# First attention: a conditioning slice's reciprocal computed by logarithm, exponential and one Newton step in place of VectorE's reciprocal instruction

## The chip, the cores and the metric

One program on one core of one Trainium2 chip. The core's engines are TensorE (PE), VectorE (DVE), ScalarE (ACT), GpSimd (POOL) and SyncE (SP), each with its own instruction stream, kept in step by semaphores. The metric is the time of one execution on the device in microseconds (us), as the median over the runs.

## The reference

The program is two layers over a batch of B = 4 sequences of T = 256 tokens with C = 256 channels. Each layer is an attention and a mixture-of-experts block, and ahead of each of these four stands a conditioning. All four conditionings have the same form, and the change touches only it:

```python
decay = exp(-exp(w))[None, :] * (0.5 + 0.5 * tf[:, :, 0])
ek    = exp(minimum(k, 30.0));  ekv = ek * v
a     = a * decay + ekv_t;      b = b * decay + ek_t      # scans, forward and in reverse
euk   = exp(minimum(u + k, 30.0))
num   = nf + nb - ekv + euk * v
den   = df + db - ek + euk
out   = sigmoid(x) * (num / maximum(den, 1e-8)) * (0.8 + 0.2 * tf)
```

Here k = v = a side input of the program, the same for all four, so `num / den` for every conditioning and sequence is known long before the `x` that it gates. `x + attention(conditioned x)` then follows. The first attention has 16 heads; its logits are mixed across heads before the softmax and its probabilities after it, by weights computed per token ("cross head projection").

## The kernel before, in words

**Slices.** A slice is one conditioning i of one sequence b: slice n = 4i + b, 16 in all. Its data are [128 x 512] in fp32 (two channel halves by 256 tokens). `slice_steps` (L971) gives VectorE's work on a slice as a list of steps: `shifted` (u + k, L987), two `forward` scans (L993), two `backward` scans (L999), `own_term` (L1021), `floor` (the maximum with 1e-8, L1033), four `invert` (a RECIPROCAL of 128 x 128 each, L1040) and `finish` (L1045), which writes num * scale * (1/den) into `fac`. ScalarE takes the exponential of `shifted` (`exp_slice`, L611), and GpSimd adds the sums (`sum_slice`, L528 to L533). `condition_batch` (L1079) multiplies `fac` with the sigmoid of x and so makes `xc`, the input of a sequence's attention.

**Who does what when.** Slice 0 is done at the start. Slices 1 to 8 are spread over the first attention, which takes one sequence b at a time: slice 2b+1 (`own`) is begun and finished in sequence b, slice 2b+2 (`following`) is begun at its end and finished in sequence b+1, where it is called `split`. Slices 9 to 15 are done later, in the expert block.

**The loop over pairs of heads.** Within a sequence a loop over p = 0..8 handles heads 2p and 2p+1. It is a software pipeline written out by hand, once in every engine's program. For pair p:

- TensorE: `second_terms` (the mixed logits), `turn` of the pair before (transposes of probabilities, L1916; it waits for `normalise`), `scores` of the next pair (it waits for VectorE's `first_rank`), `values` of the pair before (it waits for `turn_out`).
- VectorE: `first_rank` (L1199), `fold_values` (L1179), `maximum` (L1209), `mix` of the pair before (L1226), the small `invert` of row sums (L1231, waits for `exps`), and then what the dictionary `extra` has for this p: one to three steps of the slices.
- ScalarE: `turn_out` of the pair before (L701), `diagonals_pre` (L659), `exps` (L677, L679; it waits for `maximum`), `second_rank` (L686), `normalise` (L693), and at p = 4 (p = 1 in the first sequence) `exp_slice`.

Every engine runs its instructions in program order, so a wait or a long piece in one engine's pair holds back everything behind it on that engine. After p = 8 comes a sequence's tail: copies of transposed mixed probabilities (L1279, `mixqT`), the rest of slice `own` (`late_own`), the output products (L1285 to L1298), ScalarE's evacuation of values (L738) and the projections of the next sequence. `hidden0` on TensorE is the first product of the next sequence and waits for `xc`.

Function tables: ScalarE's activation functions need a table in the engine; the build puts an ACT_TABLE_LOAD ahead of an activation whose function is not in the loaded one. Before the change there are 12 such loads in the whole program; in the first attention one for the Gelu (L632) and one for the next Exp (L677) per sequence.

Of the kernel before, what the change touches and what calls it, by code (L numbers as in the profile page):

```python
# [15 lines left out]
ALU = mybir.AluOpType  # L16
ACT = mybir.ActivationFunctionType
# [3 lines left out]
B, T, C = 4, 256, 256  # L21
# [4 lines left out]
N0, HD0 = 16, 16  # L26
# [79 lines left out]
def build(nc, d, out, slots0, made0, slots, split1, made1):  # L106
    ctx = ExitStack()
    with ctx:
        def sb(name, *shape, dt=F32):
            return ctx.enter_context(nc.sbuf_tensor(name, [P, *shape], dt))  # L110

        def sem(name):
            return ctx.enter_context(nc.semaphore(name))
# [6 lines left out]
        euk, euv, num, den, backn, backd = (sb(n, CT, T) for n in ("euk", "euv", "num", "den", "backn", "backd"))  # L120
# [144 lines left out]
        c_dve, c_act = sem("cond_dve"), sem("cond_act")  # L265
# [330 lines left out]
        def _(act):  # L596
            st = Steps(act, act_own)
# [10 lines left out]
            def exp_slice(n):  # L608

                act.wait_ge(euk_in, n + 1)  # L610
                act.activation(euk[:], euk[:], ACT.Exp).then_inc(euk_out, 1)  # L611

            exp_slice(0)
            def sigmoid_batch(b):
                if b:
                    act.wait_ge(xc_ready, b)
                act.activation(sig[:], xT[:, :, bass.ds(b * T, T)], ACT.Tanh, scale=0.5).then_inc(sig_ready, 1)
# [18 lines left out]
            for b in range(B):  # L636
                for tt in range(TT):
# [6 lines left out]
                    q, k = (qk[:, tt, n].rearrange("p (n h) -> p n h", h=HD0) for n in range(2))  # L644
# [9 lines left out]
                def diagonals_pre(n):  # L654
                    if n >= 4:
                        act.wait_ge(s_ready, b * N0 + n - 3)
                    for tt in range(TT):
                        for i in range(2):
                            ins = act.activation(diag_pre[:, n % 4, 2 * tt + i], ident[:], ACT.Copy,  # L659
                                                 scale=mixw[:, tt, 1, 2 + i, n:n + 1])  # L660
                    ins.then_inc(dg_pre, 1)
# [7 lines left out]
                def exps(n):  # L669
                    s = n % 2  # L670
                    act.wait_ge(lmax, b * N0 + n + 1)
                    if n >= 2:
                        act.wait_ge(r_ready, b * N0 + n - 1)
                    if n >= 3:
                        act.wait_ge(h_done, b * N0 + n - 2)
                        act.wait_ge(t_ready, b * N0 + n - 2)
                    act.activation(prob[:, n % 3, 0:P], logit[:, s, 0:P], ACT.Exp, bias=nmax[:, s, 0:1], scale=-1.0,  # L677
                                   accum_out=rsum[:, s, 0:1])
                    act.activation(prob[:, n % 3, P:], logit[:, s, P:], ACT.Exp, bias=nmax[:, s, 1:2], scale=-1.0,  # L679
                                   accum_out=rsum[:, s, 1:2]).then_inc(p_exp, 1)  # L680
# [16 lines left out]
                def turn_out(n):  # L697
                    act.wait_ge(t_ready, b * N0 + n + 1)
                    if n >= 4:
                        act.wait_ge(pv_done, b * N0 + n // 4 * 4 - 1)  # L700
                    act.activation(probT[:, n % 4], ps[:, 2 + n % 2, 0:384], ACT.Copy).then_inc(t_read, 1)  # L701
# [6 lines left out]
                for p in range(N0 // 2 + 1):  # L708
                    pair = (2 * p, 2 * p + 1)
                    if p:  # L710
                        turn_out(2 * p - 2)
                        turn_out(2 * p - 1)
                    if 2 * p + 3 < N0:
                        diagonals_pre(2 * p + 3)
                    for n in pair:
                        if n < N0:
                            exps(n)
                    if p == 0:
                        normalise(0)
                        normalise(1)  # L720
                    for n in pair:
                        if n + 2 < N0:
                            second_rank(n + 2)
                    if p == 0:
                        diagonals_pre(4)
                    for n in pair:
                        if p and n < N0:
                            normalise(n)
                            if n % 2 == 0 and n + 4 < N0:
                                diagonals_pre(n + 4)  # L730
                    if p == (4 if b else 1):
                        exp_slice(2 * b + 1)

                exp_slice(2 * b + 2)
                if 0 < b < B - 1:
# [136 lines left out]
            for i in range(2 * B):  # L872
                b, half = divmod(i, 2)
# [73 lines left out]
        def _(dve):  # L947
            st = Steps(dve, dve_own)
# [19 lines left out]
            cs(dve.tensor_tensor(ekv[:, :, 0:T], ek[:, :, 0:T], kT[:, :, 0:T], ALU.mult))  # L968
            cs.settle()

            def slice_steps(n, nth, early=False, first=False):  # L971

# [1 line left out]
                i, b = divmod(n, B)  # L976
                cols = slice(b * T, (b + 1) * T)

                done = {}
# [50 lines left out]
                def floor():  # L1030
                    if not early and not first:
                        dve.wait_ge(sums_out, nth + 1)
                    st(dve.tensor_scalar(den[:], den[:], 1e-8, None, ALU.max))  # L1033
                    done["floor"] = st.last

                def invert(q):
                    if q == 0:
                        dve.wait_ge(*done["floor"])
                    part = den[:, q // 2, (q % 2) * P:(q % 2 + 1) * P]
                    st(dve.reciprocal(part, part))  # L1040
                    done["invert"] = st.last
# [23 lines left out]
                if first:  # L1065
# [2 lines left out]
                            lambda: finish_first(0), lambda: invert(2), lambda: invert(3), lambda: finish_first(1)]  # L1068
                return [*([] if early else [shifted]), lambda: forward(num, ekv), lambda: forward(den, ek),
                        lambda: backward(backn, ekv), lambda: backward(backd, ek),  # L1070
                        *([early_own_term, early_sums] if early else [own_term]), floor, *(lambda q=q: invert(q) for q in range(4)), finish]

            for step in slice_steps(0, 0, first=True):
                step()
# [12 lines left out]
            split = []  # L1087
# [20 lines left out]
            for b in range(B):  # L1108
# [6 lines left out]
                def heads(ap):  # L1115
                    return ap.rearrange("p (n h) -> p n h", h=HD0)
# [28 lines left out]
                for tt in range(TT):  # L1145
                    q, k = heads(qk[:, tt, 0]), heads(qk[:, tt, 1])
# [82 lines left out]
                def invert(n):  # L1229
                    dve.wait_ge(p_exp, b * N0 + n + 1)  # L1230
                    st.tell(dve.reciprocal(rinv[:, n % 2], rsum[:, n % 2]), r_ready, b * N0 + n + 1)  # L1231


                own, following = slice_steps(2 * b + 1, 2 * b + 1), slice_steps(2 * b + 2, 2 * b + 2)
                if b:
                    extra = {1: split[6:8], 2: split[8:11], 3: split[11:12] + own[0:2], 4: own[2:3], 5: own[3:4],
                             6: own[4:6], 7: own[6:8] + following[0:1]}
                else:
                    extra = {0: own[0:1], 1: own[1:2], 2: own[2:3], 3: own[3:4], 4: own[4:5], 5: own[5:6],
                             7: own[6:9] + following[0:1]}  # L1240
                for p in range(N0 // 2 + 1):
                    if p < N0 // 2:
                        first_rank(2 * p)
                        if p:
                            fold_values(2 * p)
                        dve.wait_ge(s_read, b * N0 + 2 * p + 1)
                        first_rank(2 * p + 1)
                        maximum(2 * p)
                        dve.wait_ge(s_read, b * N0 + 2 * p + 2)
                    if p == N0 // 2 and b == 0:  # L1250
                        for step in own[9:12]:
                            step()
                        condition_batch(1, 0, 2)
                    if p:
                        mix(2 * p - 2)
                    else:
                        fold_values(0)
                    if p < N0 // 2:
                        maximum(2 * p + 1)
                        invert(2 * p)  # L1260
                    if p:
                        mix(2 * p - 1)
                    else:
                        fold_values(1)
                    if p < N0 // 2:
                        invert(2 * p + 1)
                    if 0 < p < N0 // 2:
                        fold_values(2 * p + 1)
                    for step in extra.get(p, []):
                        step()  # L1270
                    if p == 3 and 0 < b < B - 1:
                        condition_batch(b + 1, 0, b + 2)

                late_own = own[8:12] if b else []
                for step in late_own[0:1]:
                    step()
                for i in range(2):
# [21 lines left out]
                split = following  # L1299
# [341 lines left out]
            first, middle, last = slice(0, HEAD), slice(HEAD, HEAD + TT), slice(HEAD + TT, TAU)  # L1641
# [17 lines left out]
            for i in range(2 * B):  # L1659
                b, half = divmod(i, 2)  # L1660
# [76 lines left out]
            for kind, which in kinds:  # L1737
                n = which.stop - which.start
# [774 lines left out]
```

## Time and profile before

| | |
|---|---|
| median of 3 runs | 1050.88 us (1050.41 to 1057.42) |
| the profiled execution | 1054.82 us, its span 1053.0 us |
| TensorE / VectorE / ScalarE busy | 913.4 / 797.4 / 572.9 us (87 / 76 / 54% of the span) |
| mean granted TensorE clock | 0.945 |
| first attention | about 20 to 440 us of the span |

The span is what the trace covers; 1.8 us of the execution lie around it. Busy shares are averages over stages with different limits. [...]

### The profile page before, as it was taken

The page shows a single profiled execution, that of the slowest core. Times are in us where ns is not written, and L with a number is a line of the kernel's source. Part 1 is how long each engine was busy: PE and PEld are TensorE (multiplying, and loading weights), DVE is VectorE, ACT ScalarE, POOL GpSimd, SP SyncE. Part 2 cuts the span into 40 slices and gives each one's busy share as a digit, 9 for nine tenths or more (in the row PEclk, how much of TensorE's full clock was granted, in tenths as well). Part 3 has the DMA queues.
Part 4 walks back from the last instruction along what each step waited for, and adds up shares of the span by engine and source line. Part 5 has one row for each costly group of instructions (what it writes and reads, how often), then busy time and mean ns, then how long its engine had stood idle before and what let it go on. Part 6 is the DMA issues. An engine that isn't in the chain of part 4 may idle for free.

```text
span 1053.0 us, 18249 instructions
## 1 busy us (share of the span) xinstructions
PE 913.4 (87%) x6216; PEld 656.6 (62%) x6216; DVE 797.4 (76%) x2089; ACT 572.9 (54%) x1458; POOL 191.2 (18%) x168
## 2 busy tenths in 40 slices
PE   2989988988898889679999999788898998899993
PEld 1777676867686777454566666523333437788983
DVE  7689889988988899984299996557666766366664
ACT  2698489838973798241233332246474761555551
POOL 1102030103001301037344443200000005011111
PEclk9999999989999999779999999969998987799997
DMA  9999950000000000035467784424464544788773
GB/s 247 199 204 237 239 141 1 2 1 1 1 2 1 1 1 2 1 124 177 133 204 242 237 250 135 173 81 164 178 218 160 210 174 138 268 324 295 275 271 130
DMA packets 71452, 153.80 MB, mean 146 GB/s; under 512 B 11439, under 2 KB 53054, under 8 KB 67136
## 3 DMA queue, kind: packets, MB, share of 16 engines
q1 hardware_dynamic: 65696, 139.93, 44.2%
q0 software_dynamic: 5664, 12.71, 3.3%
q8 instruction: 50, 0.82, 0.3%
q14 instruction: 42, 0.34, 0.1%
HBM read 122.09 MB, written 62.19 MB: 175 GB/s over the span
## 4 chain that ended last, share of the span: by engine, by line
PE 53%; DVE 25%; ACT 8%; DMA 6%; issue 5%; POOL 1%; SPq 1%; DVEq 0%; ACTq 0%; POOLq 0%
PE ps L1796 48%; DVE arena L1546 2%; DVE arena L1209 2%; DMA arena<-slots 2%; DVE arena L1199 2%; DVE arena L1226 2%; DMA arena<-split 2%; ACT arena L693 2%; POOL slots L582 1%; ACT arena L659 1%; ACT arena L686 1%; DMA made<-arena 1%; DVE arena L1179 1%; DVE arena L1775 1%; DVE den L1040 1%
## 5 line engine op out<-in xcount | busy, mean ns | idle before, releaser
L1796 PE MATMUL ps<-arena 128*128 128x128 f32 (+15 forms) x4652 | 711.4, 333 | 39.8 <-DVE arena L1199 16.2
L1796 PEld LDWEIGHTS ps<-arena 128*128 128x128 f32 (+7 forms) x4652 | 489.2, 149 | 189.1 <-issue 88.0
L1546 DVE TENSOR_REDUCE arena<-ps 128x4 f16<-128x1024 f32 (+1 forms) x48 | 58.8, 1227 | 52.5 <-PE ps L1796 52.5
L1226 DVE SCALAR_TENSOR_TENSOR arena<-arena 128x128 f32<-128x128 f32 x240 | 91.8, 442 | 0.4
L1773 DVE CAST arena<-arena 128x128 f16<-128x128 f32 (+1 forms) x128 | 33.2, 259 | 62.9 <-ACT arena L919 60.3
L659 ACT ACTIVATE arena<-ident,arena 128x128 f32<-128x128 f32 x256 | 80.2, 392 | 0.0
L824 ACT ACTIVATE arena<-ps 128x1024 f32<-128x1024 f32 x48 | 49.2, 1025 | 45.6 <-PE ps L1796 45.5
L919 ACT ACTIVATE arena<-ps,arena 128x128 f32<-128x128 f32 (+1 forms) x128 | 50.1, 417 | 44.0 <-PE ps L1796 38.8
L562 POOL DMA_INDIRECT made<-arena x47 | 53.0, 1128 | 87.0 <-DVE arena L1459 85.5
L528 POOL TENSOR_TENSOR den<-den,backd 128x512 f32<-128x512 f32 x8 | 11.9, 1482 | 280.7 <-DVE euv L1021 232.6
L1040 DVE RECIPROCAL den<-den 128x128 f32<-128x128 f32 x64 | 57.6, 928 | 0.4
L1199 DVE SCALAR_TENSOR_TENSOR arena<-arena,ps 128x128 f32<-128x128 f32 (+1 forms) x128 | 46.2, 401 | 14.3 <-PE ps L1796 13.9
L582 POOL DMA_INDIRECT slots<-side x16 | 15.6, 973 | 209.6 <-DVE side L1635 205.3
L693 ACT ACTIVATE arena<-arena 128x128 f32<-128x128 f32 (+1 forms) x128 | 49.2, 440 | 0.0
L1179 DVE TENSOR_TENSOR arena<-arena 128x512 f32<-128x512 f32 x64 | 49.0, 766 | 0.0
L1775 DVE TENSOR_TENSOR arena<-arena 128x128 f16<-128x128 f32 (+1 forms) x128 | 45.3, 354 | 4.4
L1796 PE MATMUL ps<-causal,identb 128*128 128x256 bf16 x160 | 36.7, 313 | 12.4 <-DVE arena L1546 9.7
L686 ACT ACTIVATE arena<-arena 128x128 f32<-128x128 f32 (+1 forms) x128 | 47.3, 441 | 0.1
L1576 DVE TENSOR_TENSOR arena<-arena 128x512 f16<-128x512 f32 x64 | 42.4, 683 | 5.8 <-ACT arena L864 5.7
L1916 PE MATMUL ps<-ident,arena 128*128 128x128 f32 x192 | 31.1, 285 | 17.7 <-ACT arena L693 17.1
L1209 DVE CUSTOM_DVE_ANT_0 arena<-arena 128x128 f32<-128x128 f32 (+1 forms) x128 | 46.3, 396 | 0.0
L589 POOL DMA_INDIRECT made<-arena x23 | 22.8, 990 | 128.2 <-DVE arena L1766 83.5
(301 smaller groups left out, 1234.0 us busy)
## 6 DMA issues: line engine op xcount, KB each, us to landing
arena<-split SPq DMA_DIRECT2D x15, 2048.0 KB, 9.8
arena<-in_w0all SPq DMA_DIRECT2D x32, 608.0 KB, 4.5
slots<-in_blank SPq DMA_DIRECT2D x17, 1040.0 KB, 18.7
arena<-in_w1all SPq DMA_DIRECT2D x16, 1024.0 KB, 6.9
split<-arena SPq DMA_DIRECT2D x32, 512.0 KB, 3.1
slots<-in_blank SPq DMA_DIRECT2D x10, 1044.0 KB, 23.0
arena<-slots SPq DMA_DIRECT2D x47, 130.0 KB, 3.1
side<-made SPq DMA_DIRECT2D x8, 512.0 KB, 5.7
```

Of the source, the lines that this page charges most:

```text
L562: pool.indirect_dma_start(made0[:], bass.IndirectOffsetOnAxis(ap=ids, axis=0), y0[:, j % Y0N], None, bounds_check=K0 * NT - 1, oob_is_err= ...
L659: ins = act.activation(diag_pre[:, n % 4, 2 * tt + i], ident[:], ACT.Copy, scale=mixw[:, tt, 1, 2 + i, n:n + 1])
L686: ins = act.activation(second[:, n % 2, cols], rankq[:, 1, cols], ACT.Copy, scale=mixw[:, tt, 0, 3, n:n + 1])
L693: ins = act.activation(prob[:, n % 3, cols], prob[:, n % 3, cols], ACT.Copy, scale=rinv[:, n % 2, tt:tt + 1])
L1040: st(dve.reciprocal(part, part))
L1179: dve.tensor_tensor(folded[:, n % 4].rearrange("p t (n h) -> p t n h", h=HD0), v0.rearrange("p t (n h) -> p t n h", h=HD0), spread(fold[:, ...
L1199: ins = dve.scalar_tensor_tensor(logit[:, s, tiles[tt]], rankq[:, 0, tiles[tt]], mixw[:, tt, 0, 2, n:n + 1], ps[:, s, tiles[tt]], ALU.mult ...
L1209: ins = dve.tensor_tensor_reduce(logit[:, s, tiles[tt]], logit[:, s, tiles[tt]], second[:, s, tiles[tt]], -1.0, 3.0e38, ALU.add, ALU.min, ...
L1226: ins = dve.scalar_tensor_tensor(dst, prob[:, n % 3, tiles[tt]], w, dst, ALU.mult, ALU.add)
L1546: dve.tensor_reduce(out, ps[:, at:at + 2].rearrange("p j (r s) -> p j r s", r=nr), X, ALU.max, negate=True).then_inc(max1_done, 1)
L1775: st.tell(dve.tensor_tensor(dst[:, 1, m, 0:n], hfull[:, m, 0:n], dst[:, 0, m, 0:n], ALU.subtract), h_split, c + m + 1)
L1796: return pe.matmul(o, l, r, start=start, stop=stop, skip_group_check=shared)
```

## The change

For slices 1 to 7 (all that are finished inside the first attention) the four RECIPROCALs on VectorE are replaced. ScalarE's new `invert_slice` computes euv = exp(-ln(den)), and VectorE's new `refine` does one Newton step on it in two instructions over 128 x 512: first den := (-den) * euv, then den := (den + 2) * euv, which is euv * (2 - den * euv). Slice 0 and slices 8 to 15 keep the RECIPROCAL. `euv` is a buffer that exists already. The lists of steps are then dealt out anew over the pairs, since a refined slice has 10 steps instead of 12.

```diff
+            def invert_slice(n):
+                act.wait_ge(c_dve, 8 + n)
+                st(act.activation(euv[:], den[:], ACT.Ln))
+                st.settle()
+                act.activation(euv[:], euv[:], ACT.Exp, scale=-1.0).then_inc(c_act, 1)
...
                     if p == (4 if b else 1):
                         exp_slice(2 * b + 1)
+                    if b and p == 1:
+                        invert_slice(2 * b)
+                    if p == (N0 // 2 if b else 6):
+                        invert_slice(2 * b + 1)
...
+                    if refined:
+                        st.tell(dve.tensor_scalar(den[:], den[:], 1e-8, None, ALU.max), c_dve, 8 + nth)
+                        return
...
+                def refine(q):
+                    if q == 0:
+                        dve.wait_ge(c_act, 4 + nth)
+                        st(dve.scalar_tensor_tensor(den[:], den[:], -1.0, euv[:], ALU.mult, ALU.mult))
+                    else:
+                        dve.wait_ge(*done["invert"])
+                        st(dve.scalar_tensor_tensor(den[:], den[:], 2.0, euv[:], ALU.add, ALU.mult))
+                    done["invert"] = st.last
...
-                own, following = slice_steps(2 * b + 1, 2 * b + 1), slice_steps(2 * b + 2, 2 * b + 2)
+                own = slice_steps(2 * b + 1, 2 * b + 1, refined=True)
+                following = slice_steps(2 * b + 2, 2 * b + 2, refined=b < B - 1)
                 if b:
-                    extra = {1: split[6:8], 2: split[8:11], 3: split[11:12] + own[0:2], 4: own[2:3], 5: own[3:4],
-                             6: own[4:6], 7: own[6:8] + following[0:1]}
+                    extra = {1: split[6:7], 2: split[7:9], 3: split[9:10] + own[0:1], 4: own[1:2], 5: own[2:4],
+                             6: own[4:6], 7: own[6:7] + following[0:1]}
                 else:
                     extra = {0: own[0:1], 1: own[1:2], 2: own[2:3], 3: own[3:4], 4: own[4:5], 5: own[5:6],
-                             7: own[6:9] + following[0:1]}
+                             6: own[6:7], 7: own[7:9] + following[0:1]}
...
-                late_own = own[8:12] if b else []
+                late_own = own[7:10] if b else []
```

ScalarE in sequence 1 at the end of pair 1, before: the last head's `normalise`, then `turn_out`, the diagonals and `exps` of the next pair.

```order
L693 ACTIVATE arena<-arena 128x128
L693 ACTIVATE arena<-arena 128x256
L701 ACTIVATE arena<-ps 128x384 x2
L659 ACTIVATE arena<-ident,arena 128x128 x4
L677 ACTIVATE arena<-arena 128x128
L679 ACTIVATE arena<-arena 128x256
```

The same place after (L693 is now L700, L701 is L708, L659 is L666, L677 is L684):

```order
L700 ACTIVATE arena<-arena 128x128
L700 ACTIVATE arena<-arena 128x256
L616 ACT_TABLE_LOAD
L616 ACTIVATE euv<-den 128x512
L618 ACT_TABLE_LOAD
L618 ACTIVATE euv<-euv 128x512
L708 ACTIVATE arena<-ps 128x384 x2
L666 ACTIVATE arena<-ident,arena 128x128 x4
L684 ACTIVATE arena<-arena 128x128
L686 ACTIVATE arena<-arena 128x256
```

Four instructions stand between `normalise` and `turn_out`, two of them table loads. The same four stand ahead of the last but one `turn_out` pair of sequence 0 (after p = 6) and behind the last `turn_out` of sequences 1 to 3 (p = 8); the whole program has 26 table loads in place of 12.

VectorE at the end of sequence 0, before: fold of pair 7, slice 1's floor and reciprocals around slice 2's `shifted`, its finish, and `xc` of sequence 1.

```order
L1179 TENSOR_TENSOR arena<-arena 128x512
L1033 TENSOR_SCALAR den<-den 128x512
L1040 RECIPROCAL den<-den 128x128 x2
L987 TENSOR_SCALAR euk<-side,wu 128x256 x2
L1040 RECIPROCAL den<-den 128x128 x2
L1045 SCALAR_TENSOR_TENSOR fac<-num,oscale,den 128x2x256
L1079 SCALAR_TENSOR_TENSOR xc<-sig,fac 128x512
```

The same place after (L1179 is now L1205):

```order
L1205 TENSOR_TENSOR arena<-arena 128x512
L1054 SCALAR_TENSOR_TENSOR den<-den,euv 128x512
L1057 SCALAR_TENSOR_TENSOR den<-den,euv 128x512
L998 TENSOR_SCALAR euk<-side,wu 128x256 x2
L1069 SCALAR_TENSOR_TENSOR fac<-num,oscale,den 128x2x256
L1105 SCALAR_TENSOR_TENSOR xc<-sig,fac 128x512
```

Two instructions stand where four reciprocals stood, and the floor has gone to the end of pair 6, from where ScalarE waits for it.

VectorE in the tail of sequence 1, before: last `mix`, a reciprocal, the `mixqT` copies, two reciprocals, finish, the forward scan of the following slice.

```order
L1226 SCALAR_TENSOR_TENSOR arena<-arena 128x256
L1040 RECIPROCAL den<-den 128x128
L1279 COPY arena<-ps 128x384 x2
L1040 RECIPROCAL den<-den 128x128 x2
L1045 SCALAR_TENSOR_TENSOR fac<-num,oscale,den 128x2x256
L993 SCALAR_TENSOR_TENSOR num<-dec,side 128x256 x2
L1285 SCALAR_TENSOR_TENSOR arena<-arena,ps 128x256 x2
```

The same place after:

```order
L1252 SCALAR_TENSOR_TENSOR arena<-arena 128x256
L1054 SCALAR_TENSOR_TENSOR den<-den,euv 128x512
L1306 COPY arena<-ps 128x384 x2
L1057 SCALAR_TENSOR_TENSOR den<-den,euv 128x512
L1069 SCALAR_TENSOR_TENSOR fac<-num,oscale,den 128x2x256
L1004 SCALAR_TENSOR_TENSOR num<-dec,side 128x256 x2
L1312 SCALAR_TENSOR_TENSOR arena<-arena,ps 128x256 x2
```

One refining step stands ahead of the copies and one behind, where one reciprocal stood ahead and two behind.

## Rows read from the trace of the kernel before

**Rows 1.** The page: busy time by engine, and the chain that ended last.

```profile
PE 913.4 (87%) x6216; PEld 656.6 (62%) x6216; DVE 797.4 (76%) x2089; ACT 572.9 (54%) x1458; POOL 191.2 (18%) x168
PE 53%; DVE 25%; ACT 8%; DMA 6%; issue 5%; POOL 1%; SPq 1%; DVEq 0%; ACTq 0%; POOLq 0%
```

**Rows 2.** Windows, sequence 1, pairs 1 to 5: length; PE, PEld, DVE, ACT, POOL busy; clock; DMA; GB/s.

```profile
153.00:162.40 9.40, 7.90 (x58) 6.64 (x57) 9.34 (x26) 9.36 (x32) 4.14 (x4) 1.00 0.00 0
162.40:171.70 9.30, 8.16 (x70) 6.53 (x68) 8.89 (x29) 9.04 (x31) 0.00 (x0) 1.00 0.00 1
171.70:181.00 9.30, 7.76 (x58) 6.63 (x56) 9.26 (x31) 8.07 (x28) 0.00 (x0) 1.00 0.01 2
181.00:189.20 8.20, 6.68 (x55) 5.22 (x56) 7.68 (x27) 6.67 (x23) 0.00 (x0) 1.00 0.00 1
189.20:197.10 7.90, 7.67 (x59) 6.78 (x58) 7.73 (x26) 7.87 (x26) 0.00 (x0) 1.00 0.01 2
```

**Rows 3.** Groups by line and form, 0 to 480 us: busy, mean ns of one, idle before.

```profile
L1040 DVE RECIPROCAL den<-den 128x128 f32<-128x128 f32 x32 | 28.6, 926 | 0.3
L1045 DVE SCALAR_TENSOR_TENSOR fac<-num,oscale,den 128x512 f32<-128x512 f32 x7 | 5.2, 746 | 0.1
L611 ACT ACTIVATE euk<-euk 128x512 f32<-128x512 f32 x9 | 5.6, 623 | 1.7 <-DVE euk L987 1.7
L632 ACT ACT_TABLE_LOAD x4 | 5.1, 1283 | 0.1
L993 DVE TENSOR_TENSOR_SCAN den<-dec,side 128x256 f32<-128x256 f32 x18 | 12.4, 731 | 0.0
```

**Rows 4.** Timeline of ACT, sequence 1, pairs 1 to 4: start, length, instruction, idle before.

```profile
163.84 0.47 ACT L701 ACTIVATE arena<-ps 128x384 f32<-128x384 f32 x1
...
172.32 0.87 ACT L701 ACTIVATE arena<-ps 128x384 f32<-128x384 f32 x2 [0.42 <-PE ps L1916]
...
176.03 0.40 ACT L677 ACTIVATE arena<-arena 128x128 f32<-128x128 f32 x1 [0.80 <-DVE arena L1209]
...
183.61 0.40 ACT L677 ACTIVATE arena<-arena 128x128 f32<-128x128 f32 x1 [0.37 <-DVE arena L1209]
...
185.49 0.40 ACT L677 ACTIVATE arena<-arena 128x128 f32<-128x128 f32 x1 [0.89 <-DVE arena L1209]
```

**Rows 5.** Timeline of ACT, sequence 0, from `normalise` of pair 6 on.

```profile
104.31 1.48 ACT L693 ACTIVATE arena<-arena 128x128 f32<-128x128 f32 x4
105.73 0.49 ACT L701 ACTIVATE arena<-ps 128x384 f32<-128x384 f32 x1
...
108.41 0.40 ACT L677 ACTIVATE arena<-arena 128x128 f32<-128x128 f32 x1 [0.63 <-DVE arena L1209]
```

**Rows 6.** Timeline of PE, end of sequence 0: the last values, then `hidden0`.

```profile
111.96 3.65 PE L1796 MATMUL ps<-arena 128*32 128x256 f32 x28 [0.58 <-ACT arena L701]
116.24 1.99 PE L1796 MATMUL ps<-xc,arena 128*128 128x256 f32 x8 [0.63 <-DVE xc L1079]
```

**Rows 7.** Timeline of PE, sequence 1: `values` of pair 1, and the last turns.

```profile
165.64 6.32 PE L1796 MATMUL ps<-arena 128*32 128x256 f32 x52
...
215.23 1.27 PE L1916 MATMUL ps<-ident,arena 128*128 128x128 f32 x6 [1.71 <-ACT arena L693]
```

**Rows 8.** Windows of 1 us, two of sequence 1: columns as in rows 2.

```profile
216.00:217.00 1.00, 0.50 (x3) 0.23 (x3) 1.00 (x3) 0.77 (x2) 0.00 (x0) 0.65 0.00 0
...
222.00:223.00 1.00, 1.00 (x4) 0.73 (x4) 0.00 (x0) 0.00 (x0) 0.00 (x0) 0.50 0.00 0
```

**Rows 9.** Timeline of ACT and of DVE, tail of sequence 1.

```profile
219.24 1.08 ACT L632 ACTIVATE arena<-ps 128x512 f32<-128x512 f32 x2
223.67 1.02 ACT L738 ACTIVATE arena<-ps 128x1024 f32<-128x1024 f32 x1 [3.35 <-PE ps L1796]
...
224.00 1.02 DVE L1279 COPY arena<-ps 128x384 f32<-128x384 f32 x2 [3.05 <-PE ps L1965]
224.94 1.75 DVE L1040 RECIPROCAL den<-den 128x128 f32<-128x128 f32 x2
```

More of the change, by code:

```diff
@@ L969, in _, with slice_steps @@
             cs.settle()
-            def slice_steps(n, nth, early=False, first=False):
+            def slice_steps(n, nth, early=False, first=False, refined=False):
                 i, b = divmod(n, B)
@@ L1070, in slice_steps @@
                         lambda: backward(backn, ekv), lambda: backward(backd, ek),
-                        *([early_own_term, early_sums] if early else [own_term]), floor, *(lambda q=q: invert(q) for q in range(4)), finish]
+                        *([early_own_term, early_sums] if early else [own_term]), floor,
+                        *((lambda q=q: refine(q)) if refined else (lambda q=q: invert(q)) for q in range(2 if refined else 4)),
+                        finish]
             for step in slice_steps(0, 0, first=True):
@@ L1250, in _ @@
                     if p == N0 // 2 and b == 0:
-                        for step in own[9:12]:
+                        for step in own[9:10]:
                             step()
```

## Prediction

> **What bounds the kernel now.** The page first: TensorE is busy 87% of the span, VectorE 76, ScalarE 54, and the chain that ended last gives PE 53%, DVE 25%, ACT 8% [rows 1]. By these shares ScalarE looks like the engine with room. The reader has to go on to the stage that the change touches. There, in the windows by pair of heads [rows 2], the three engines stand level: in pair 1 ScalarE is busy 9.36 of 9.40 us and VectorE 9.34, in pair 2 ScalarE 9.04 of 9.30 and VectorE 8.89; only in pairs 3 and 4 has ScalarE room (8.07 of 9.30, 6.67 of 8.20), and in pair 5 none (7.87 of 7.90). The timelines of the engines come third, since they say what each gap waits for: ScalarE runs from the last `normalise` of pair 1 straight into `turn_out` at 163.84, and its gaps afterwards are short [rows 4]. So the question is less what VectorE saves than where ScalarE is given its new work.
>
> **The change part by part.**
>
> *VectorE, a slice.* Four reciprocals of 926 ns mean go; they overlap a little at their ends, and four take 3.4 to 3.5 us (a run of two 1.75 with its overlap [rows 9]). Two SCALAR_TENSOR_TENSOR of 128 x 512 come, the form of `finish`, 746 ns each [rows 3], some 1.42 together. Saved: 2.0 us for each of seven slices, 14 us of VectorE's work.
>
> *ScalarE, a slice.* Two table loads of 1283 ns and two ACTIVATEs of 128 x 512. The latter form takes 623 ns as Exp [rows 3]. Ln does not occur in the trace; bounds from the nearest rows are 0.49 us (the 128 x 384 form from `ps` [rows 5]) and 1.02 us (128 x 1024 [rows 9]), and I take 0.62. The burst is 2 x 1.283 + 2 x 0.623 = 3.8 us, with 3.7 to 4.2 as its ends. Seven bursts are 27 us of ScalarE, twice what VectorE is spared. The loads do not overlap with what is beside them: the Gelu evacuation starts at 219.24 behind a load and four such loads had 0.1 us idle before them [rows 3, 9].
>
> [...]
>
> *Sequences 1 to 3, slice 2b, pair 1.* The burst stands ahead of `turn_out` at 163.84 [rows 4], and VectorE's floor is done by then, so it costs no wait, only its length: `turn_out`, the diagonals and `exps` of pair 2 come 3.8 us late. Queued behind them: TensorE's `values` of pair 1 (the block that starts at 165.64 [rows 7]) waits for `turn_out` until about 168.5, and VectorE's small `invert` waits for `exps`, so that what it was spared in pairs 1 and 2 (0.9 and 1.1 us) is spent idle. What is late next is taken back where ScalarE had gaps: 0.80 in pair 3, 0.37 and 0.89 in pair 4 [rows 4]; that is 2.06, and the 0.42 at 172.32 becomes the wait of 0.26 that a turn behind a `normalise` always costs, 0.16 more. At most 2.2 of 3.8 are absorbed. VectorE and TensorE are late too and have their own work in these pairs, so I take 1.8 and leave 2.0 late at the end of pair 4. Pair 5 has no room: ScalarE is full [rows 2], and VectorE now has two scans where it had one (a group of two halves takes about 1.2 to 1.4 us; a half 731 ns mean [rows 3]). Walking VectorE through, it starts pair 5 some 1.8 late, waits for `exps` and leaves 3.4 late; pair 6 has its old steps, and leaves 3.0 late.
>
> *Sequences 1 to 3, slice 2b+1, pair 7 and tail.* One reciprocal less at the end of pair 7 (0.9 us) is no gain on the path, since the last `turn` waits for a `normalise` that follows `maximum`, ahead of it in VectorE's order; `values` of pair 7 starts 3.0 late. The burst after the last `turn_out` lies beside this `values` block and TensorE's transposes. ScalarE was idle 3.35 us there [rows 9]; 3.8 us more puts the evacuation at L738 about 1 us behind `values`, which TensorE covers with the transposes and the first product that it has ahead of needing it. If that cover were gone, it would cost that 1 us per sequence. VectorE's first refining step falls into its 3.05 us idle ahead of the `mixqT` copies [rows 9]. Behind the copies one step of 0.7 stands in place of two reciprocals of 1.7 [rows 9]: a gain of 1.0 on the path. Net for each of three sequences: 3.0 - 1.0 = +2.0.
>
> *Sequence 0, slice 1.* The burst stands behind `normalise` of pair 6 (ends 105.7), ahead of two `turn_out`s, with only pair 7 to come. The slack ahead of `exps` of the second head is 0.63 [rows 5], so `normalise` of heads 14 and 15 comes 3.0 to 3.2 late, and so does the last `values`, which began at 111.96 and ended at 115.6 [rows 6]. It would end near 118.8. `hidden0` of sequence 1, which started at 116.24 on `xc` [rows 6], now waits for this block, ahead of it in TensorE's order: +2.6. VectorE's side (floor moved out, four reciprocals to two steps: -2.4) no longer decides; with the wait for `exps` its `xc` comes about 1 us later than before.
>
> *TensorE's clock.* [...] The change makes four new gaps of about 3 us (pair 2 of three sequences) and 4 us (pair 7 of sequence 0). A low stretch of 3.4 us, half of the one seen, takes 1.7 us of TensorE's work; I reckon with it at two of four places: +3.4, between 0 and 4 x 3.4 = 13.6.
>
> **The sum.** 3 x 2.0 + 2.6 + 3.4 = +12.0 us. The profiled execution took 1054.82 us (span 1053.0 and 1.8 around it) and would become 1066.8. It lay 0.4% above the median of 1050.88; put on the median, the forecast is 1062.9 us. All else (projections, the expert blocks, the second layer) shifts as a whole.
>
> **The rivals.**
>
> *The burst is hidden (faster).* If the pairs have more give than I read, what remains is VectorE's saving on the path: at least 3 x 1.0 in the tails and 2.4 in sequence 0, at most also 1.1 + 0.9 + 0.9 in the pairs of each of three sequences, so -5.4 to -14.1: 1037 to 1045, say 1041. For it: ScalarE is 54% busy, and VectorE over 95% in pairs 1 to 3. Against it: ScalarE's 9.36 of 9.40. It decides the other way from the point at which ScalarE's gaps in pairs 2 to 5 exceed 3.8 us; the rows have 2.5. Chance 0.13.
>
> *The two cancel (no change).* Absorption reaches its 2.2, VectorE's savings in pairs 2 and 3 let it catch up before the double scan, no new low stretch of clock: +0.5 a sequence, +2.0 in sequence 0, about +3: 1054, with 1046 to 1060 around it. Chance 0.29.
>
> *The clock cascade (slower still).* Each new gap brings a low stretch of 6.6 us like the one of rows 8, 3.3 us of work lost at four places in place of two times 1.7: 8.6 + 13.2 = +22: 1073. For it: the stretch of rows 8 followed a gap shorter than the new ones. Against: part of it falls where TensorE waits anyway. Chance 0.08.
>
> *The forecast* (burst on the path, part absorbed, 1056 to 1070 by itself) has 0.50.
>
> **How the numbers follow.** About 1%, or 10.5 us, is what a measurement of this kernel tells from no change. Of the forecast's 0.50 some 0.38 lies above 1061.4, with the 0.08 of the cascade and 0.01 of the rest: slower 0.47. Faster takes most of the first rival, under 1040.4 to near 1045: with half of that rival's spread above the bound it is 0.10. Same has the remaining 0.43. The range runs from 1046, which leaves out the hidden burst, to 1074, which takes in the cascade and a burst of 4.2 us.
>
> **What would show it.** Right: two ACT_TABLE_LOADs at each of seven places, and ScalarE's `turn_out` of pair 2 starting about 3.8 us later relative to the last `normalise`; VectorE waiting 2 to 3 us for `exps` (L684/L686 there) in pair 2 and in pair 7 of sequence 0, where it had 0.4 or nothing; TensorE idle about 3 us ahead of `values` of pair 1; sequence length up by about 2 us, with the tail 1 us shorter than before. Wrong: loads that cost nothing beside other work, pairs 2 to 4 no longer than before, or `hidden0` starting before 116.2; then the first or second rival holds. A cascade would show as stretches of 0.50 in the clock behind each of the new gaps.

## The result and the profile after

| | before | after |
|---|---|---|
| median of 20 runs each, us | 1053.52 (1050.18 to 1058.2) | 1061.52 (1055.28 to 1065.13) |
| ratio after / before | | 1.0073, 95% interval 1.0058 to 1.0089 |
| profiled execution, us | 1054.82 | 1065.13, its span 1063.3 |
| mean granted TensorE clock | 0.945 | 0.940 |

The kernel became slower by 0.7%, some 8 us. The forecast was slower by 12.0 us with a range from 1046 to 1074: direction and range were right, the amount half as large again as measured. The profiled execution of the change is the slowest of its 20, 3.6 us above their median, and that of before lies 1.3 us above its own, so the two profiles differ by more (10.3 us) than the medians.

The page's busy times, as in [rows 1]:

```profile
PE 915.8 (86%) x6216; PEld 657.9 (62%) x6216; DVE 784.1 (74%) x2075; ACT 598.5 (56%) x1486; POOL 191.6 (18%) x168
PE 52%; DVE 23%; ACT 10%; DMA 7%; issue 5%; SPq 1%; POOL 1%; ACTq 0%; DVEq 0%; POOLq 0%
```

VectorE has lost 13.3 us of work and ScalarE has gained 25.6; ScalarE's share of the chain rose from 8 to 10%. The groups by form answer to [rows 3]:

```profile
L616 ACT ACT_TABLE_LOAD x7 | 9.0, 1283 | 0.1
L618 ACT ACT_TABLE_LOAD x7 | 9.0, 1283 | 0.1
L616 ACT ACTIVATE euv<-den 128x512 f32<-128x512 f32 x7 | 4.4, 630 | 0.1
L1054 DVE SCALAR_TENSOR_TENSOR den<-den,euv 128x512 f32<-128x512 f32 x7 | 4.8, 687 | 5.5 <-ACT euv L618 5.5
L1257 DVE RECIPROCAL arena<-arena 128x2 f32<-128x2 f32 x64 | 10.1, 158 | 22.0 <-ACT arena L686 21.6
```

Every price was as taken: loads of 1283 ns with nothing beside them, Ln 630 ns. The last row shows where VectorE's savings went: ahead of the small reciprocal of row sums, which waits for `exps`, VectorE stood idle for 7.6 us in all before the change and for 22.0 now. Pair 1 to 2 of sequence 1, ScalarE (compare [rows 4]), VectorE, and TensorE (compare [rows 7]):

```profile
168.61 0.78 ACT L700 ACTIVATE arena<-arena 128x128 f32<-128x128 f32 x2
169.41 1.28 ACT L616 ACT_TABLE_LOAD   x1
170.71 0.63 ACT L616 ACTIVATE euv<-den 128x512 f32<-128x512 f32 x1
171.36 1.28 ACT L618 ACT_TABLE_LOAD   x1
172.65 0.63 ACT L618 ACTIVATE euv<-euv 128x512 f32<-128x512 f32 x1
173.19 0.85 ACT L708 ACTIVATE arena<-ps 128x384 f32<-128x384 f32 x2
```

```profile
176.10 0.17 DVE L1257 RECIPROCAL arena<-arena 128x2 f32<-128x2 f32 x1 [4.81 <-ACT arena L686]
```

```profile
174.09 8.22 PE L1823 MATMUL ps<-arena 128*32 128x256 f32 x52 [2.92 <-ACT arena L708]
```

From the end of `normalise` to `turn_out` ScalarE needs 3.80 us where it needed none. VectorE waits 4.81 us in one piece, TensorE 2.92 us; and TensorE's block of 52 products then takes 8.22 us where it took 6.32: the granted clock is at 0.50 of full speed from 171.3 us, just after the gap begins, to 178.1. Windows of 1 us (columns as in [rows 2]) at this place, and the end of sequence 0 on TensorE (compare [rows 6]):

```profile
173.00:174.00 1.00, 0.00 (x0) 0.00 (x0) 0.00 (x0) 1.00 (x4) 0.00 (x0) 0.50 0.00 0
...
176.00:177.00 1.00, 1.00 (x4) 0.73 (x4) 0.90 (x4) 1.00 (x6) 0.00 (x0) 0.50 0.00 0
```

```profile
111.77 5.25 PE L1823 MATMUL ps<-arena 128*128 128x256 f32 x12 [4.09 <-ACT arena L708]
116.86 0.82 PE L1943 MATMUL ps<-ident,arena 128*128 128x128 f32 x6
118.31 3.64 PE L1823 MATMUL ps<-arena 128*32 128x256 f32 x28 [0.64 <-ACT arena L708]
```

In sequence 0 the gap is 4.09 us, and the 12 products behind it take 5.25 us in place of 2.86. A good mark for a sequence's end are the `mixqT` copies on VectorE (L1279 before, L1306 after). They start at 120.32, 224.00, 330.67 and 433.69 us before and at 125.78, 231.66, 336.73 and 445.10 after. In these two executions sequence 1 is 2.2 us longer and sequence 3 5.4, while sequence 2 is 1.6 shorter, in part because the profile of before has a low stretch of clock in its middle (from 288 us, 6.8 us long; the block of 52 products behind it takes 8.71 us). So one pair of profiles does not size the parts; the experiments have to.

### The profile page after: what moved, and what is told of

It reads as the page before. It is cut to its first block, busy times and chain, and to the rows that moved or that the text cites. A ratio compares the mean times of both kernels' runs of the same rounds, so it can differ in the third digit from the quotient of the medians.

```text
span 1063.3 us, 18263 instructions
## 1 busy us (share of the span) xinstructions
PE 915.8 (86%) x6216; PEld 657.9 (62%) x6216; DVE 784.1 (74%) x2075; ACT 598.5 (56%) x1486; POOL 191.6 (18%) x168
## 4 chain that ended last, share of the span: by engine, by line
PE 52%; DVE 23%; ACT 10%; DMA 7%; issue 5%; SPq 1%; POOL 1%; ACTq 0%; DVEq 0%; POOLq 0%
PE ps L1823 47%; DMA arena<-slots 2%; DVE arena L1225 2%; DVE arena L1573 2%; DMA arena<-split 2%; DMA made<-arena 2%; DVE arena L1235 2%; DVE arena L1252 2%; POOL slots L582 1%; DVE arena L1205 1%; ACT arena L700 1%; DVE arena L1802 1%; ACT arena L693 1%; SPq L363 1%; ACT L616 1%
## 5 line engine op out<-in xcount | busy, mean ns | idle before, releaser
L666 ACT ACTIVATE arena<-ident,arena 128x128 f32<-128x128 f32 x256 | 80.3, 393 | 0.0
L700 ACT ACTIVATE arena<-arena 128x128 f32<-128x128 f32 (+1 forms) x128 | 49.3, 442 | 0.1
L1205 DVE TENSOR_TENSOR arena<-arena 128x512 f32<-128x512 f32 x64 | 49.0, 766 | 0.0
L693 ACT ACTIVATE arena<-arena 128x128 f32<-128x128 f32 (+1 forms) x128 | 47.4, 441 | 0.1
L684 ACT ACTIVATE arena<-arena 128x128 f32<-128x128 f32 x64 | 25.4, 397 | 26.3 <-DVE arena L1235 26.0
```

The source lines that it names most:

```text
L693: ins = act.activation(second[:, n % 2, cols], rankq[:, 1, cols], ACT.Copy, scale=mixw[:, tt, 0, 3, n:n + 1])
L700: ins = act.activation(prob[:, n % 3, cols], prob[:, n % 3, cols], ACT.Copy, scale=rinv[:, n % 2, tt:tt + 1])
L1205: dve.tensor_tensor(folded[:, n % 4].rearrange("p t (n h) -> p t n h", h=HD0), v0.rearrange("p t (n h) -> p t n h", h=HD0), spread(fold[:, ...
```

## The experiments

Twelve kernels ran, in three sets on two other chips. The kernel before took 1065 to 1066 us there (medians of 31 to 35 runs a set); ratios are against it in the same set, and are not the quotients of the medians, from which they differ by up to 0.3%. Lengths are told by the copies that end a sequence; for the profiles, the sum of sequences 1 to 3 and how long the clock was at its lower level in them is:

| profile | sequences 1 to 3, us | of it at 0.50, us | ratio in the runs |
|---|---|---|---|
| before (first profile) | 313.4 | 23.9 | 1 |
| the change (first profile, f1) | 319.3, 319.5 | 27.3, 27.3 | 1.0073, 1.0058 |
| e1 (tail bursts alone) | 314.4 | 37.5 | 1.0013 |
| e2 (no burst in pair 1) | 313.5 | 34.1 | 1.0019 |
| e3 (six loads fewer) | 314.3 | 23.9 | 0.9994 |
| e4, f2 (change, filled) | 313.9, 315.7 | 10.2, 17.1 | 1.0032, 1.0019 |
| f3 (pair 1 bursts alone) | 317.8 | 23.9 | 1.0063 |
| f4 (scans not moved) | 323.3 | 41.0 | 1.0075 |
| g3 (f3, filled) | 310.8 | 6.8 | 0.9976 |
| g1 (before, filled) | 305.7 | 10.2 | 0.9932 |
| g2 (tail bursts, filled) | 308.4 | 10.2 | 0.9940 |
| g4 (change, filled twice) | 315.9 | 10.2 | 1.0051 |

Rows with like time at 0.50 can be compared for the lag alone (how much later the waits make the engines, with the clock left out): g4, g2, g1 and e4. Each row is one execution, and these are not all typical: f1's profile is the slowest of its twelve, 6.4 us above their median, g1's lies 5.5 below its own. The kernel before has no profile on these two chips. What follows the copies of sequence 3, where the kernels do nearly the same work, took 624.4 to 633.8 us in these profiles and 619.3 and 618.2 in the first two, so a total carries several us that the change did not make. "Filled" kernels have products of 128 x 128 into a bank that is unused at that time; nothing reads them.

**e1, only the bursts in the tails.** In `extra`, `late_own` and the two programs slices 3, 5 and 7 are refined (the dictionary `RANK` names them), all others as before; on ScalarE:

```diff
+RANK = {3: 1, 5: 2, 7: 3}
...
-                    if b and p == 1:
+                    if b and p == 1 and 2 * b in RANK:
                         invert_slice(2 * b)
-                    if p == (N0 // 2 if b else 6):
+                    if p == (N0 // 2 if b else 6) and 2 * b + 1 in RANK:
                         invert_slice(2 * b + 1)
```

> Only slices 3, 5 and 7 are refined (their burst stands behind the last turn_out of sequences 1 to 3); slices 1, 2, 4 and 6 keep the four reciprocals and the steps are dealt out as in the kernel before. Theory (a burst costs only where ScalarE has no idle time to lay it in): the burst lies beside the last block of values, VectorE's tail is 1.0 us shorter in each of three sequences, so about 3 us faster than before, 1.5 to 4, and the mixqT copies start no later than before. Rival (a burst costs the pipeline wherever it stands, here by the late evacuation at L738): no gain or a loss, 0 to +3 us against before.

Measured: 1.0013 (0.9984 to 1.0041), no gain. The tails themselves are shorter: from the copies to the next sequence's small reduction 11.01 us in sequences 1 and 2, before 12.07 and 12.06. The interval does not exclude a gain of up to 1.7 us, the low end of what was expected; the expected 3 it does. The last values of sequence 1 run at the lower clock here (0.50 from 218.7 to 225.5 us):

```profile
219.80 6.40 PE L1824 MATMUL ps<-arena 128*32 128x256 f32 x28 [0.58 <-ACT arena L709]
```

g2 shows what becomes of the shorter tail when they do not.

**e2, no burst in pair 1.** As e1, and slice 1 is refined too.

> Slices 1, 3, 5 and 7 are refined, slices 2, 4 and 6 (the burst in pair 1) are not. Against e1 it adds only sequence 0's burst after pair 6. Theory: that burst costs 2.6 us of lag and a stretch of low clock behind the 4 us gap on TensorE, so 3 to 5 us slower than e1, and about 0 to +2 against before; against the full change some 6 to 9 us faster, since three bursts in pair 1 are gone. Rival (the loss is in sequence 0 alone): equal to the full change, +7 against before.

Measured: 1.0019 (0.9989 to 1.0049). The copies of sequence 0 start at 124.41 us, 4.1 later than before, as with the full change in f1 (124.10). Against before (+2 to +3 us, 0 to +2 expected) this is near what was expected; in the medians it is 2 us above e1, where 3 to 5 were expected, within the noise of both. It is 4 to 6 us better than the full change by the ratios, where 6 to 9 were expected.

**e3, three bursts without table loads.** For slices 1, 2 and 3 the kernel leaves out the logarithm; the instructions are as many and as large otherwise:

```diff
-                st(act.activation(euv[:], den[:], ACT.Ln))
+                st(act.activation(euv[:], den[:], ACT.Copy if n < 4 else ACT.Ln))
```

> The full change, but for slices 1, 2 and 3 the Ln is replaced by a Copy, which needs no table of its own: the three bursts are 1.25 us in place of 3.8 (6 of 14 table loads gone). It leaves out the logarithm of these slices, so their conditioning is near zero; the instructions are as many and as large otherwise. Theory: in sequence 0 the last values block starts within 1 us of where it did before the change, with no stretch of low clock ahead of it, and in sequence 1 TensorE waits 0.3 us or less for turn_out ahead of the values of pair 1 in place of 2.9; sequences 0 and 1 together come 6 to 10 us shorter than in the full change (some 2.5 x 2 of lag and the low clock), sequences 2 and 3 as in the full change: +0 to +3 against before. Rival (not the loads but the wait of one engine for another or the moved scans cost the time): the stage stays within 1 us of the full change.

Measured: 0.9994 (0.9965 to 1.0023). It is level with before, where 0 to +3 us were expected. Sequence 0 ends at 119.77, 0.55 before the old mark, and sequence 1 at 221.24, which is 10.4 us before the full change's mark in its first profile and 7.3 before that of f1, where 6 to 10 were expected. On TensorE the values of pair 1 wait 0.22 us:

```profile
165.40 7.92 PE L1823 MATMUL ps<-arena 128*32 128x256 f32 x52 [0.22 <-ACT arena L708]
```

So a burst of two ACTIVATEs at these places costs nothing that the profile shows; six table loads of 1283 ns, with the gaps and the low clock that come with them, make the difference in these two sequences. The clock is not tied to the new gap alone, though: here the block of values takes 7.92 us in place of 6.32, with the clock at 0.50 from 165.4 to 168.8, and TensorE's longest idle time just ahead of it is 1.14 us, as in the kernel before.

**e4 and f2, the gaps that the bursts open filled.** Ahead of TensorE's wait for `turn_out`:

```diff
                 def values(p):
+                    if p == (1 if b else 6):
+                        for _ in range(11):
+                            mm(ps[:, 7, 0:P], dw1[:, 0, 0:P], ident[:])
                     pe.wait_ge(t_read, b * N0 + 2 * p + 2)
```

> The full change, with 11 products of 128 x 128 into an unused bank placed on TensorE right before it waits for turn_out in the values of pair 1 (sequences 1 to 3) and of pair 6 (sequence 0): they fill the gaps of 3 to 4 us that the burst opens, and nothing reads them. Theory that the lower clock after these gaps is part of the loss: no stretch of 0.50 follows them, the values block behind takes 6.3 us in place of 8.2 and 2.9 in place of 5.2, and the kernel is 2 to 6 us faster than the full change, +2 to +6 against before. Rival (the clock only falls where TensorE has slack anyway): as the full change, +7, or slower by what the added products cost (up to 3 us each).

Measured: 1.0032 (0.9999 to 1.0066), within the +2 to +6 us expected. The same places as above, now with the filling products (11 of them, 22 MATMULs and 2.62 us in the trace) and the clock kept up (1.00 from 104 to 124 us and from 160 to 180):

```profile
105.69 2.62 PE L1824 MATMUL ps<-ident,arena 128*128 128x128 f32 x22
109.95 2.86 PE L1824 MATMUL ps<-arena 128*128 128x256 f32 x12 [1.64 <-ACT arena L709]
...
167.05 2.62 PE L1824 MATMUL ps<-ident,arena 128*128 128x128 f32 x22
170.13 6.32 PE L1824 MATMUL ps<-arena 128*32 128x256 f32 x52 [0.46 <-ACT arena L709]
```

The blocks are back at 2.86 and 6.32 us. Sequence 0 ends at 121.83: of the 4.1 us that its burst costs in e2, 1.5 are lag and 2.6 the clock (f1: 2.3).

**f1, the change itself beside the others.**

> The changed kernel itself, for comparison with the others on one chip (a chip other than the first gave the kernel before 1065 us in the first set of experiments). Theory: slower than before by 0.4 to 1.1%, as on record. Rival (the 7.7 us were the clock's luck on the first chip): within 0.3% of before, like e1 to e4.

Measured: 1.0058 (1.0037 to 1.0079): the first result repeats on another chip.

> The kernel of e4 once more, beside the full change on the same chip. Its profile showed no low clock behind the four gaps and sequences 0 and 1 shorter by 4.0 and 2.5 us than in the full change. Theory (low stretches behind the new gaps are part of the loss): 2 to 6 us faster than the full change beside it. Rival (a low stretch avoided here comes back later, since the kernel as a whole idles as much): within 2 us of it.

Measured: 1.0019 (0.9999 to 1.0040), 4 us less than f1, with intervals that only just meet. The clock's part of the loss is seen here in the total; g4, which has the same fillings and more, does not bear that out (1.0051).

**f3, only the bursts in pair 1.** Slices 2, 4 and 6 refined.

> Only slices 2, 4 and 6 are refined, with the burst in pair 1 of sequences 1 to 3; slices 1, 3, 5 and 7 keep the reciprocals. Theory: each burst leaves about 3 us of lag (no tail gain here) and a low stretch behind TensorE's 2.9 us gap, so +6 to +10 us against before, and more than the 4 to 5 us of sequence 0's burst alone (e2 less e1). Rival (pair 1's burst is absorbed and sequence 0 carries the loss): 0 to +3 us.

Measured: 1.0063 (1.0043 to 1.0082). As expected, +7.0 us in the medians, at least as much as the full change.

**f4, the scans where they were.**

```diff
-                    extra = {1: split[6:7], 2: split[7:9], 3: split[9:10] + own[0:1], 4: own[1:2], 5: own[2:4],
+                    extra = {1: split[6:7], 2: split[7:9], 3: split[9:10] + own[0:2], 4: own[2:3], 5: own[3:4],
```

> The full change, but in sequences 1 to 3 slice 2b+1's scans stay in the pairs where they were (two steps in pair 3, one in 4, one in 5). Theory (the double scan of pair 5 adds about 1 us a sequence, since VectorE is the late engine there): sequences 1 to 3 each 0.5 to 1.5 us shorter in the profile, 1.5 to 4 us faster than the full change. Rival (pair 3 is where VectorE is late now, after its 4.8 us wait in pair 2, so a scan there costs as much): equal to the full change or slower by up to 2 us.

Measured: 1.0075 (1.0047 to 1.0104), against f1's 1.0058 (1.0037 to 1.0079). The rival was right in that nothing is gained: after its wait of 4.82 us in pair 2 VectorE is late in pair 3, and a scan there makes TensorE's scores wait 1.66 us behind that pair, where the change has 0.50:

```profile
192.79 0.92 PE L1823 MATMUL ps<-arena 32*128 32x128 f32 x8 [1.66 <-DVE arena L1225]
```

The moved scan is no part of the loss. Whether it helped is not settled: f4 is 4.9 us above f1 in the medians but 1.8 by the ratios, the intervals overlap, and its profile has 13.7 us more of low clock.

**g1, the kernel before with gaps filled.**

```diff
+                def fill(count, bank):
+                    for _ in range(count):
+                        mm(ps[:, bank, 0:P], dw1[:, 0, 0:P], ident[:])
...
+                    if b and p == N0 // 2:
+                        pe.wait_ge(s_read, b * N0 + N0)
+                        fill(6, 0)
                     if p:
                         turn(2 * p - 2)
                         turn(2 * p - 1)
+                    if b and p == N0 // 2:
+                        fill(2, 0)
+                    if b and p == 4:
+                        fill(5, 7)
```

> The kernel before, with products that nothing reads laid into three gaps of TensorE that it has in sequences 1 to 3: 5 ahead of the scores of pair 5, 6 ahead of the last turns and 2 ahead of the last values. No slice is changed. Theory (a low stretch of clock behind a gap is on the path, here as in the full change): the stretches of 0.50 at the end of sequences 1 to 3 (6.8, 3.4, 6.8 us in the profile of before) are gone, 1.5 to 3 us each, so 3 to 8 us faster than before. Rival (they move elsewhere): within 2 us of before.

Measured: 0.9932 (0.9902 to 0.9961), 1060.01 us against 1066.00. Faster than both kernels. At the end of sequence 1 the last values take 3.65 us; in the kernel before they took 6.56, most of it at the low clock (0.50 from 216.3 to 223.1 us, in g1 1.00 throughout the tail). First that row of before, then g1:

```profile
217.08 6.56 PE L1796 MATMUL ps<-arena 128*32 128x256 f32 x28 [0.58 <-ACT arena L701]
```

```profile
214.88 1.50 PE L1796 MATMUL ps<-ident,arena 128*128 128x128 f32 x12
216.76 1.24 PE L1916 MATMUL ps<-ident,arena 128*128 128x128 f32 x6 [0.38 <-ACT arena L693]
217.83 0.61 PE L1796 MATMUL ps<-ident,arena 128*128 128x128 f32 x4
218.58 3.65 PE L1796 MATMUL ps<-arena 128*32 128x256 f32 x28
```

And ScalarE's evacuation of these values, for which it stood idle 3.35 us before [rows 9], now has 0.40:

```profile
222.26 1.02 ACT L738 ACTIVATE arena<-ps 128x1024 f32<-128x1024 f32 x1 [0.40 <-PE ps L1796]
```

So most of the room that a burst in the tail was to be laid in was made by the low clock.

**g2, e1 with the same gaps filled.**

> e1 (slices 3, 5 and 7 refined) with the same filled gaps as g1. Theory: e1's tails are 0.5 to 1 us shorter each once the clock does not hide it, so 1 to 3 us faster than g1 and faster than both kernels. Rival (e1's gain is nothing): equal to g1.

Measured: 0.9940 (0.9917 to 0.9963): equal to g1 in the runs, the rival (its one profile has sequences 1 to 3 longer than g1's by 2.7 us). TensorE's and ScalarE's timelines in the tail of sequence 1 say why:

```profile
221.74 1.88 PE L1824 MATMUL ps<-arena,xc 128*128 128x512 f32 x4
225.32 1.09 PE L2011 MATMUL ps<-ident,arena 128*128 128x128 f32 x8 [1.70 <-ACT arena L750]
```

```profile
217.56 1.28 ACT L617 ACT_TABLE_LOAD   x1
...
223.26 1.09 ACT L640 ACTIVATE arena<-ps 128x512 f32<-128x512 f32 x2
224.23 1.03 ACT L750 ACTIVATE arena<-ps 128x1024 f32<-128x1024 f32 x1
```

With the clock up (1.00 from 214 to 228 us), the last values take 3.65 us in place of e1's 6.40, and now the evacuation at L750, queued behind the burst and the Gelu, is late: TensorE waits 1.70 us for it. From the copies to the next reduction it is 12.47 us, against 12.07 in g1. Only where a low clock stretches the values is the evacuation in time: in all profiles with a full burst of 3.8 us in the tail, it is 11.01 us long behind values of 6.40 us or more, 11.3 to 11.5 behind 5.1 to 5.3, and about 12.47 behind 3.65. The f1 profile has the same wait of 1.70 in sequences 1 and 2, the one after the change in sequence 2 and 0.24 in sequence 1.

**g3, f3 with its gap filled.**

> f3 (slices 2, 4 and 6 refined, +7 us) with 11 products laid into the gap of 2.9 us in pair 1 of sequences 1 to 3. Theory: of the 7 us about 3 x 1.0 to 1.5 are the clock and the rest is the lag of the burst, so +3 to +5 against before. Rival (all of it is lag): +7; rival (all of it is clock): 0.

Measured: 0.9976 (0.9950 to 1.0003), so the theory (+3 to +5) missed, and it is nearest to the rival that all is clock: 0.87% less than f3 (compared through the kernel before, since they ran in different sets), which is more than the whole of f3's loss. It is not all clock, though: it lies above g1 by 0.44%, with intervals that overlap, and in its profile sequence 2 is 104.0 us long with no low stretch, in g1 102.2 with one of 3.4 us.

**g4, the full change with both fillings.**

> The full change with both sets of filled gaps (those of e4 and those of g1). Theory: with the clock kept up on both sides what is left between this and g1 is the lag alone: sequence 0 1.5 us, sequences 1 to 3 1 to 2 us each, so 4 to 7 us slower than g1 and about level with before. Rival (the lag was only ever the clock): level with g1.

Measured: 1.0051 (1.0028 to 1.0073), 10 us above g1 where 4 to 7 were expected, and 4 above before where level was expected. The profiles agree: with equal time at the lower clock over the three together, sequences 1, 2 and 3 are 3.0, 3.1 and 4.0 us longer than g1's, 10.1 in all; the split is less sure, since the low stretches fall in different sequences. That is the lag without the clock, and it is the 3.0 of the walk with nothing taken off for the tail, which is itself 0.4 longer twice; g3 less g1 puts 1.7 a sequence of it on the burst of pair 1, as an estimate, since their fillings differ. Why g1's fillings help the kernel before and not f2 is open: the two profiles are equal up to the end of the first attention (315.9 and 315.7), and the intervals of the ratios overlap.

## Why the prediction was right, and where its sizes were off

*ScalarE has no room in pair 1, though it is 54% busy.* Right, and the base of the rest. The burst took 3.80 us, and `turn_out` came that much later.

*What waits.* TensorE's gaps of about 3 and 4 us were 2.92 and 4.09. VectorE's wait for `exps` was given as 2 to 3 us in pair 2; it was 4.81 there, 0.41 before (2.62 in sequence 0). The 4.40 more are the burst's 3.80 and most likely part of the time that VectorE was spared, which it spends idle.

*Sequence 0, +2.6 and its clock.* The lag alone is +1.5 at the copies (e4), the low clock adds 2.3 to 2.6 (f1, e2 against e4). The term of 2.6 was for the lag, with the clock counted elsewhere, so it was 1.1 too high; both together are 4.1.

*The bursts of sequences 1 to 3.* The walk gave 3.0 of lag ahead of the tail, and g4 against g1 has 3.0, 3.1 and 4.0, tails included. The wait of 0.26 us in it is what three places of sequence 1 show before the change (0.26, 0.27 and 0.26 us, `turn_out` at 164.56, 181.59 and 199.42), not what a turn always costs: at 216.53 it is 0.23, at 207.18 it is 1.58. The bursts of pair 1 carry the loss: f3 alone is +7.0 in the medians, f1 +5.9. All of f3's loss goes when its gap is filled (g3), but the kernel before gains by fillings too (g1), so this does not make the loss clock alone.

*The tail's gain of 1.0 a sequence.* This is the step that failed. VectorE's own tail is 1.06 us shorter (12.07 to 11.01), but I named a cover for the late evacuation at L738, the transposes and first product on TensorE, and it holds only where the last values run at the low clock. The 3.35 us of ScalarE's idle time [rows 9] from which the burst was to be paid were read in a sequence whose last values ran that way, 6.56 us long; with the clock up there are 0.40 (g1), and then TensorE waits 1.70 us and the tail is 0.4 longer than before. After the change sequence 1 had 11.48 and sequence 2 12.47: -0.6 and +0.4, nothing on balance in place of -2.

*The double scan in pair 5.* Priced as part of the lag; f4 shows that undoing it gains nothing.

*The clock, +3.4 from two of four gaps.* The stretch of which 3.4 us is half is that of [rows 8], in the kernel before: the granted clock at 0.50 from 216.3 to 223.1 us, behind 1.71 us of idle time on TensorE and 1.27 of work. No run shows the +3.4 itself, which was an estimate. In the first profile of the change a low stretch begins within or at the end of each of the four gaps, 6.8 us long in sequences 0 and 1, 3.4 in the others (f4 has one gap, of 2.29 us, without). Yet the whole time at 0.50 in sequences 1 to 3 rose only from 23.9 to 27.3 us, since the kernel before has its own stretches elsewhere, and where it is slowed by them the lag hides. So the term was of the right kind but its price, a new stretch of low clock simply added, was not: some stretches came in place of others.

*The price of a load.* It was 1283 ns and no more, as the rows of before said: Ln starts 1.30 us after the start of the load before it, and ScalarE stood idle 0.1 us in all before the seven loads of each line. All seven places had two loads, 26 in the whole program; in e3, where a Copy stands for the Ln at three of them, these three had none, and the program has 20.

*The sum.* 12.0 forecast, 8.0 between the medians of 20 runs. The missing gain of the tails alone would have made it worse, so lag and clock together (15.0) were sized about 7 us too high for a kernel whose clock falls anyway: with gaps filled on both sides the change costs 10.1 us between the medians (g4 less g1), more than the 8.0 and 5.9 measured without. How the 7 us split over the terms stays open; the intervals of the runs are 3 to 7 us wide. That the forecast time, 1062.9 us, lies only 1.4 from the measured 1061.52 is in part luck: the median of before that it started from was of 3 runs, and the 20 runs put it 2.6 us higher.

## What to carry to other kernels

A share of the span says nothing of a stage (54% of it for ScalarE, and 9.36 of 9.40 us in pair 1): move work to the engine that has gaps in the pair of rows where the work will stand, and count its table loads (here 2.6 of 3.8 us a burst). Work put ahead of what two other engines wait for opened gaps on TensorE here, and one was charged twice, as a wait (2.92 us) and as a stretch at a granted clock of 0.50 (8.22 us for a block that took 6.32). Where such a gap cannot be avoided, a few products that nobody reads, placed ahead of the wait, can pay: on the kernel before they gave 0.7%, on the change 0.4% in one pair of kernels (f1, f2) and next to nothing in another (f1, g4). And room read in a profile is room only at the clock of that profile (ScalarE's 3.35 us were 0.40 in g1, with the clock at 1.00): look at the granted clock of the rows before laying work into an idle time.

## What was not expected of the hardware

Idle gaps of 0.6 to 1.7 us on TensorE (4.26 at the end of sequence 3), which the kernel before has in plenty, are in part followed by 3.4 or 6.8 us at a granted clock of 0.50, and 13 small products a sequence laid at three such places made that kernel 0.7% faster (0.4 to 1.0). The same unchanged kernel had medians of 1053.5, 1065.1 and 1066.1 us on three chips, further apart than the change moved it, so that only ratios within a set can be read.
